# Single-bank scores and 512-column exponentials in a two-layer attention kernel

## What is computed

```python
def layer0(x, emb, mask, ...):              # 16 heads
    xn = layer_norm(x)
    q, k = heads(xn @ q_w + q_b), heads(xn @ k_w + k_b)
    att = softmax(q . k + (1 - mask_of_row) * -1e6, over the keys)
    y = att @ heads((xn @ v_w + v_b) * mask)
    scale, shift = split(silu(emb) @ emb_w + emb_b)
    h = layer_norm(y) * (1 + scale) + shift
    return x + silu(h) @ out_w + out_b
def layer1(x, emb, mask, ...):              # 8 heads
    q = softmax(xn @ Wq + bq, over channels of a head)
    k = softmax(xn @ Wk + bk + (1 - mask) * -1e6, over tokens)
    y = q @ (k^T @ v) per head              # then as in layer 0
```

## Time and profile before

| | |
|---|---|
| median of 3 runs | 665.94 us (665.83 to 666.95) |
| the profiled execution: time / span | 663.26 us / 661.5 us |
| mean granted TensorE clock | 0.933 of full speed |
| TensorE (products) busy | 568.3 us, 86% |
| VectorE busy | 446.4 us, 67% |
| ScalarE busy | 334.5 us, 51% |

### The profile page before, as it was taken

One profiled execution on the slowest core, in us unless ns is written; L12 is line 12 of the kernel. 1 busy time (PEld: TensorE's weight loads), 2 busy tenths in 40 slices (PEclk: granted clock), 3 DMA queues, 4 the chain that ended last, 5 costly groups with the idle time before them and its releaser, 6 DMA issues.

```text
span 661.5 us, 7870 instructions
## 1 busy us (share of the span) xinstructions
PE 568.3 (86%) x2938; PEld 273.5 (41%) x2938; DVE 446.4 (67%) x899; ACT 334.5 (51%) x399; POOL 66.7 (10%) x86
## 2 busy tenths in 40 slices
PE   3528789999999999989999988999889899956966
PEld 2214342333533344444334434554335443514755
DVE  5246854766599988768998866768885785222552
ACT  3111064554566665547667544555575456651430
POOL 2040050000000212000020400000421020002100
PEclk9769779999999998999999988999899899996888
DMA  6378930546200030303030000011001000000001
GB/s 185 77 202 216 270 115 0 131 117 153 63 26 17 11 75 1 75 0 75 2 74 25 2 25 1 1 28 35 20 23 34 33 2 1 1 1 0 0 1 63
DMA packets 18557, 36.14 MB, mean 55 GB/s; under 512 B 3956, under 2 KB 10476, under 8 KB 17496
## 3 DMA queue, kind: packets, MB, share of 16 engines
q1 hardware_dynamic: 18432, 35.62, 21.3%
q10 hardware_dynamic: 88, 0.02, 0.0%
HBM read 20.50 MB, written 14.70 MB: 53 GB/s over the span
## 4 chain that ended last, share of the span: by engine, by line
PE 60%; DVE 26%; DMA 4%; issue 3%; ACT 3%; SPq 3%; POOL 0%; POOLq 0%; DVEq 0%; ACTq 0%
DVE halfmax L993 16%; PE bank L860 16%; PE bank L749 14%; PE bank L728 8%; PE sT L728 4%; PE bank L801 3%; PE sT L841 3%; PE bank L770 2%; DVE stats L912 2%; PE bank L763 2%; PE bank L758 1%; ACT prob L692 1%; DVE xs L1037 1%; PE bank L822 1%; DMA qs<-stack_rows 1%
## 5 line engine op out<-in xcount | busy, mean ns | idle before, releaser
L993 DVE TENSOR_REDUCE halfmax<-bank 128x1 f32<-128x512 f32 x512 | 319.3, 682 | 72.5 <-PE bank L749 71.0
L692 ACT ACTIVATE prob<-sT 128x1024 f32<-128x1024 f32 x256 | 247.7, 1024 | 155.0 <-PE sT L841 154.3
L749 PE MATMUL bank<-ks,qs 50*128 50x512 f32 x512 | 196.8, 498 | 45.4 <-DVE halfmax L993 23.1
L749 PEld LDWEIGHTS bank<-ks,qs 50*128 50x128 f32 x512 | 79.3, 189 | 179.1 <-DVE halfmax L993 114.1
L860 PE MATMUL bank<-prob,vp 128*17 128x512 f32 x1024 | 139.7, 618 | 0.6 <-ACT prob L692 0.6
L841 PE MATMUL sT<-qs,ks 52*128 52x512 f32 x512 | 97.2, 415 | 5.7 <-DMA qs<-crows 3.7
L554 POOL TENSOR_TENSOR rstd<-var,neghalf 128x4 f32<-128x4 f32 x14 | 14.2, 1013 | 535.5 <-DVE var L922 535.5
L841 PEld LDWEIGHTS sT<-qs,ks 52*128 52x128 f32 x512 | 53.1, 190 | 19.7 <-ACT prob L692 8.4
L728 PE MATMUL bank<-w,hT 128*128 128x256 f32 x144 | 38.8, 406 | 0.0
L728 PEld LDWEIGHTS bank<-w,hT 128*128 128x128 f32 x144 | 27.0, 204 | 13.9 <-DVE halfmax L993 8.3
L860 PEld LDWEIGHTS bank<-prob,vp 128*17 128x17 f32 x1024 | 17.0, 95 | 34.1 <-issue 24.8
(11 more groups left out here) (133 smaller groups left out, 468.5 us busy)
## 6 DMA issues: line engine op xcount, KB each, us to landing
stack_rows<-late SPq DMA_DIRECT2D x16, 512.0 KB, 6.7
ks<-stack_rows SPq DMA_DIRECT2D x16, 384.0 KB
qs<-stack_rows SPq DMA_DIRECT2D x32, 192.0 KB, 3.4
stack_rows<-late SPq DMA_DIRECT2D x16, 256.0 KB, 5.7
out_x<-xs SPq DMA_DIRECT2D x4, 512.0 KB, 2.9
xs<-in_x SPq DMA_DIRECT2D x4, 256.0 KB, 3.9
xs<-in_x SPq DMA_DIRECT2D x2, 512.0 KB, 5.6
late<-in_L_cond_emb_w SPq DMA_DIRECT2D x1, 1024.0 KB, 8.4
```

The lines of the kernel that those rows point to most:

```text
L692: act.activation(prob[:, c % 2, 2 * u:2 * u + 2, :].rearrange("p j n -> p (j n)"), sT[u][:, :], ACT.Exp).then_inc(exp_done, 1)
L749: last = pe.matmul(o, qs[rows, s % SLOTS, c, t * P:(t + 1) * P], ks[rows, hg, c, half * HALF:(half + 1) * HALF], start=True, stop=True)
L993: dve.tensor_reduce(halfmax[:, s % 2, r, half:half + 1], o, axis=AX.X, op=ALU.max, negate=True).then_inc(u.done, 1)
```

## The change

- PSUM is eight single banks. Banks 0 to 2 are for scores, used in turn, one product each; the exponential is one activation of 512 columns a head, four a step instead of two. Product number n of the loop waits for exponential n - 3. Bank 3 joins the ring of maxima and units, which has four banks now. The prologue's units have three banks instead of four, the end section's seven instead of eight.
- The order on TensorE in a step is: scores 0 and 1, maxima (first share), `values(k - 1)`, maxima (second share), scores 2 and 3, maxima (third share), units. VectorE does the first two shares, `dve_mid`, the third share, `dve_at`.
- `places` chooses the shares by the step's units. With the numbers of this kernel, every step up to 117 still has four maxima: 3, 1, 0 in steps without a unit or with one small one, 2, 2, 0 in steps with a large unit, 3, 0, 1 in steps with two small ones.
- In the end section the output products of each half follow the transposes of that half; VectorE does the third `y1` between the statistics and the scaling of the first half's normalisation; and `keep_busy` adds products whose result nobody reads, into bank 7: five after the last `y`, four after the last `out0`, three after the last `y1`.

```diff
-        sT = [ctx.enter_context(nc.psum_tensor(f"sT{i}", [P, 2 * HALF], F32)) for i in range(2)]
...
-        acc = B8[4]
+        B8 = [ctx.enter_context(nc.psum_tensor(f"bank{i}", [P, HALF], F32))[:, :] for i in range(8)]
+        score_banks, acc = B8[0:3], B8[4]
...
+        def places(k):
+            kinds = [key[0] for key in pe_at[k]]
+            if any(kind not in SMALL and kind not in ("y", "neg") for kind in kinds):
+                return [2, 2, 0]
+            return [2, 0, 1] if len(kinds) > 1 else [2, 1, 0]
+
+        LEAD, MOST = 2, 4
+        runs, taken_to = [], AHEAD
+        for k in range(STEPS):
+            s, c = divmod(k, NT)
+            count = places(k)
+            most = min(len(stream), MAXES * (s + 2 + int(c >= 3))) - taken_to
+            least = max(min(len(stream), MAXES * ((k + f + 1 + LEAD) // NT + 1)) - taken_to - MOST * f for f in range(min(2 * NT, STEPS - k)))
+            total = max(min(sum(count), most), min(least, MOST))
+            for place_of in (2, 1, 0):
+                while sum(count) > total and count[place_of] > 0:
+                    count[place_of] -= 1
+            for place_of, limit in ((0, 3), (2, 3), (1, 3)):
+                while sum(count) < total and count[place_of] < limit:
+                    count[place_of] += 1
...
-            return maxima(k, 0) + dve_mid[k] + maxima(k, 1) + dve_at[k]
+            return maxima(k, 0) + maxima(k, 1) + dve_mid[k] + maxima(k, 2) + dve_at[k]
...
-            end_order += [("T", "mid1", b, h, kc) for kc in range(KC)]
-        end_order += [("out1", b, s) for s in range(4)]
+            end_order += [("T", "mid1", b, h, kc) for kc in range(KC)] + [("out1", b, 2 * h + i) for i in range(2)]
...
-        dve_end += [("y1", b, 0), ("y1", b, 1)] + dve_layer("mid1", 0) + [("y1", b, 2), ("y1", b, 3)] + dve_layer("mid1", 1)
+        norm = dve_layer("mid1", 0)
+        dve_end += [("y1", b, 0), ("y1", b, 1)] + norm[:-1] + [("y1", b, 2)] + norm[-1:] + [("y1", b, 3)] + dve_layer("mid1", 1)
...
-        place(pro_order, B8[0:4], pro_ready, [key for key in pro_order if key[0] in ON_ACT], [key for key in pro_order if key[0] == "qk"], pro_act, pro_dve)
-        place(in_ring, B8[5:8], ring_ready, act_order, dve_order, ring_act, ring_dve, taken)
-        place(end_order, B8[0:8], end_ready, [key for key in act_end if key in end_order], [key for key in dve_end if key in end_order], end_act, end_dve)
+        place(pro_order, B8[0:3], pro_ready, [key for key in pro_order if key[0] in ON_ACT], [key for key in pro_order if key[0] == "qk"], pro_act, pro_dve)
+        place(in_ring, [B8[3]] + B8[5:8], ring_ready, act_order, dve_order, ring_act, ring_dve, taken)
+        place(end_order, B8[0:7], end_ready, [key for key in act_end if key in end_order], [key for key in dve_end if key in end_order], end_act, end_dve)
...
-            def exponential(k, u):
+            def exponential(k, j):
                 s, c = where(k)
-                act.wait_ge(sT_ready, 2 * k + u + 1)
-                if u == 0 and k >= 2:
+                use = GH * k + j
+                act.wait_ge(sT_ready, use + 1)
+                if j == 0 and k >= 2:
                     act.wait_ge(pv_done, k - 1)
-                act.activation(prob[:, c % 2, 2 * u:2 * u + 2, :].rearrange("p j n -> p (j n)"), sT[u][:, :], ACT.Exp).then_inc(exp_done, 1)
+                act.activation(prob[:, c % 2, j, :], score_banks[use % len(score_banks)], ACT.Exp).then_inc(exp_done, 1)
...
-                if k > 0:
-                    pe.wait_ge(exp_done, 2 * (k - 1) + u + 1)
...
+                use = GH * k + j
+                if use >= len(score_banks):
+                    pe.wait_ge(exp_done, use - len(score_banks) + 1)
+                rows = slice(two * TILE, two * TILE + ROWS)
+                pe.matmul(score_banks[use % len(score_banks)], ks[rows, hg, u, c * P:(c + 1) * P],
+                          qs[rows, s % SLOTS, u, :], start=True, stop=True).then_inc(sT_ready, 1)
...
-                for key in maxima(k, 0):
-                    fill(key)
                 scores(k, 0)
                 scores(k, 1)
-                for key in maxima(k, 1):
+                for key in maxima(k, 0):
                     fill(key)
                 if k > 0:
                     values(k - 1)
+                for key in maxima(k, 1):
+                    fill(key)
+                scores(k, 2)
+                scores(k, 3)
+                for key in maxima(k, 2):
+                    fill(key)
                 for key in pe_at[k]:
                     fill(key)
             values(STEPS - 1)
+            def keep_busy(n):
+
+                for i in range(n):
+                    pe.matmul(B8[7], ident[:, :], wv0[:, :, :].rearrange("p k d -> p (k d)"), start=True, stop=True)
+
+            busy = {("y", SUBS - 1): 5, ("out0", b, 3): 4, ("y1", b, 3): 3}
```

43 lines of the change are left out of this document (21 added, 22 removed).

## The result

| | before | after |
|---|---|---|
| median of 4 runs each | 665.88 us | 632.95 us (628.19 to 635.09) |
| ratio, 95% interval | | 0.9498 [0.944, 0.9556] |
| the profiled execution: time / span | 663.26 / 661.5 us | 633.4 / 631.6 us |
| mean granted TensorE clock | 0.933 | 0.949 |

What follows compares the result with a forecast made beforehand. The bound was a wait for a bank between TensorE and VectorE, not an engine. Loop -17.3 and end -7 made -24.3: 639.0 us for the profiled execution, plus 2.7 for the median, 642; range 628 to 662, leaving out the slower case.

Steps and rivals of the forecast that it cites:

- `qk`, without step 15: Loop steps with a qk unit: 5.20 to 4.40 us with no bank wait left, eight steps, -6.4 us.
- plain, 22: Plain steps without other VectorE work: +0.38 us each, +8.3; four with the `acc` copy a further 0.25, +1.0.
- plain with statistics or other VectorE work, 10: Ten plain loop steps already long by VectorE's work, which hides the new 3.07 us: 0.
- `neg`: Nine loop steps with `neg`: from 2.91 to 3.07 us, +1.4 us.
- without maxima, 5: Last loop steps, without maxima: from 1.93 to 2.66 us, 0.73 each, +3.6 us.
- 79 to 81: Loop stretch of dropped clock: 21.65 to 15.7 us, -6; bounds nothing and -7.6.
- 100 to 109: Loop stretch of dropped clock: 47.17 to 41.2 us, -6; bounds nothing and -8.5.
- prologue / end section: Prologue 0, bounds -1.5 to +1; end section -7 from full clock and reordering, bounds -11.3 and +3.
- the rival of 679 us: Slower case: clock drops in plain steps, 1.85 us more each; 679 us at 20 such steps; chance 0.16.
- my circle of 3.07: Plain step set by score 1 waiting for score 2's exponential: 3.07 us, 0.38 more than now.
- The wait for the first maxima's DMA: Loop start: DMA queued behind the embedding weights in either kernel, 3.7 us of waiting; prologue change put at 0.
- a late DMA of the maxima: Maxima's DMA coming late for score 0: costs 0, since score 1 waits anyway.

Runs made afterwards that it cites:

- the run with three: Changed kernel with three banks instead of four in the ring of maxima and units, one bank idle: 670.99 us, ratio to before 1.0028.
- the one order: Changed kernel with SyncE issuing the next sub-block's maxima load ahead of the query and key stores: 627.48 us, ratio 0.9418.
- the one addition: Changed kernel with GpSimd's second-layer output bias addition cut into eight pieces: 627.24 us, ratio 0.9431.
- the combined kernel: Changed kernel plus earlier first maxima load, score 1 behind first maxima, maxima load before stores, bias addition in pieces, added products before the loop: 616.78 us, 0.927.

## Why the prediction was right, and where its sizes were off

The step periods of both kernels, summed by kind (us, changed minus before), beside the prediction's terms:

| steps | forecast | measured |
|---|---|---|
| `qk`, without step 15 | -6.4 (8 steps) | -6.0 (7) |
| `v`, `values`, without step 16 | -1.7 | -1.5 |
| keys, out0, `y1` | -4.9 | -5.0 |
| queries | -3.7 | -3.8 |
| `y` alone | -1.5 | -1.7 |
| emb, att, single transposes | -1.4 | -2.3 |
| two transposes (T, T) | 0 | -1.4 |
| plain, 22 | +9.3 | +7.7 |
| plain with statistics or other VectorE work, 10 | 0 | -6.0 |
| plain with the maximum's pieces, 4 | 0 | -0.4 |
| `neg` | +1.4 | -0.6 |
| without maxima, 5 | +3.6 | +3.2 |
| 79 to 81 | -6 | -5.7 |
| 100 to 109 | -6 | -7.1 |
| 1, 2 / 15, 16 / 78 | 0 | +2.3 / +2.7 / +2.1 |
| prologue / end section | 0 / -7 | +1.9 / -8.5 |

Two rows of the table need reading. The pairs of transposes stayed as forecast (3.72 before, 3.75 after, in four of six); 1.15 of their 1.4 us is step 77, which in the kernel before paid for the cast held by GpSimd. And the plain steps come near the forecast by two errors that cancel in part: 14 of them lost only 0.2 us each instead of 0.38, while the four with the copy of `acc` lost 0.50 and four others 0.6 to 0.8.

**Right.** That the bank between TensorE and VectorE set the steps, and that the fourth ring bank removes it where a unit stands: shown by the run with three. That the plain step would be set by score 1 waiting for the exponential of score 2: shown by the timeline and by moving score 1; loads of L868 wait 65.4 us for ScalarE, 25 or more were forecast. That ScalarE's longer work is hidden: shown in the kernel before. The clock stayed at 1.00 in plain steps, though TensorE's products now stand for 0.48 us in each (7.15 us busy of 8.60); the rival of 679 us fell. What the Trainium skill (TensorE: Matmul & The Clock Gate, A second HAM failure mode) reports of a kernel whose products cycle through PSUM banks, and the prediction weighed as that rival, did not come here: the trace does not agree (clock 1.00 from 199.03 to 207.63).

**Mis-sized terms.** The largest is the ten plain steps with statistics, which I put at 0 because VectorE has more than a step of work there. It has, but with four banks TensorE no longer waits when VectorE lags: the first such step takes 2.87 us, with VectorE busy throughout, against 3.70. The `neg` steps, forecast at 3.07, mostly stayed as they were: eight of eleven take 2.85 to 2.98 (2.90 and 2.91 before), and two gained 0.47 each. In the plain step my circle of 3.07 has two terms too long: from the fourth maximum to the exponential it takes 0.57 (0.11 + 0.58 in the forecast), since score 2 goes out beside it, and from score 1 to the values 0.66 (0.3 + 0.42); 0.99 + 0.57 + 0.65 + 0.66 = 2.87. The plain steps thus came out at 2.87, outside the 3.0 to 3.1 that I named. `qk` steps came out at 4.23, not 4.40: the two groups of four products take 0.66 and 0.67 us, not 0.76 each (0.98 + 0.66 + 1.92 + 0.67).

**Not foreseen.** The wait for the first maxima's DMA, which I took as unchanged, became 11.5 us, and behind it steps 1 and 2 run at a clock of 0.60 and are 2.3 us longer than before. That this comes of the wait is not shown: with the first load ahead they take the same 10.8 us. At the start of a sub I had put a late DMA of the maxima at 0, since score 1 waits anyway; in three plain steps it costs 0.4 to 0.6 us beyond the 2.87. In step 15 the faster loop ran into SyncE's four stores, which the change does not touch; in the kernel before they were issued by 152.90 and the maxima ready at 155.24. The hold by GpSimd's addition is not new, as the row of the kernel before shows: it cost 1.2 us there in step 77 and 2.2 in step 78 here. The runs with the one order or the one addition changed show these two. In the end section the gain at full clock came (out0 and keys -3.3 and -2.7), and `y1` and the last outputs give -3.9 of the 4.6 forecast. But the five products ran partly at half clock and ended at 575.8, 10.6 us behind the last values, where the first transposes of the kernel before started 8.0 behind them.

**The sum.** Forecast -24.3 for the span, measured -29.9. That the two are no further apart is partly luck: what I had not foreseen lost 9.0 us (the start of the loop, steps 1, 2, 15, 16 and 78), and what I had put at 0 or at a loss gained about as much (the statistics steps -6.0, `neg` 2.0 better than forecast, step 77 -1.2). The other 3 us between 642 and 632.95 come from the medians: I added 2.7 for how that of the kernel before stands to its profiled execution, while the changed kernel's stands 0.45 below. What stays open: why the clock falls at one place in one kernel and not in another whose order is the same there (step 9 in the combined kernel, steps 16 and 79 and the last values in some and not in others).

## What to carry to other kernels

Count banks by the wait that they end: one more bank for the engine that lags was worth 5% here, the same bank for scores nothing that the runs can tell. Where two engines hand banks to each other, look at the order in the queue as well as at the number: moving one product behind those that need not wait took 0.18 us off each plain step. After a speed-up, look again at every DMA issue and every long GpSimd instruction that the faster stage now meets, and size added products by their own row.

## What the runs showed of the hardware

- A cast of 128x16 took 3.54 us on VectorE beside a GpSimd addition over 2048 elements, 0.36 beside the same addition in eight pieces, 0.17 alone. The instruction behind it, of two inputs in SBUF, took 0.66 beside the pieces and 0.18 alone; a reduction from PSUM took 0.68 beside the whole addition, as elsewhere.
- With two neighbouring products in different halves of the rows it took 0.57 us from the maximum's load to the exponential, with both in the same half 0.77.
- A 128x512 product of full f32 on 128 rows took 0.87 us at full clock, four times one on 50 rows of the maxima's kind (0.22). Rows and type differ together, so which of them it is stays open.
- Plain steps with TensorE's products standing 0.48 us of 2.87 kept the granted clock at 1.00. At the end of the loop, after five steps without maxima and a wait of 1.2 us for the last exponential, it fell within 2.4 us of the last values in nine of the twelve kernels with the new order, and not in three.
